# A Mamba-2 mixer with a LoRA mixture layer: all y and B of paired groups turned by VectorE, and its order beside GpSimd's splits rewritten

## The reference

```python
x = hidden; xn = layernorm(x)
proj = xn @ in_proj_w.T                    # gate 4096 | x 4096, B 1024, C 1024 | dt 64
xBC = silu(causal_conv4(hbc))              # 4 taps along time
dt_p = softplus(dt + dt_bias); dA = exp(dt_p * -exp(A_log))
state = state * dA + (dt_p * x) B^T        # per head (64 heads of 64, 8 groups, N = 128)
y = state C + x * D
yn = y * rsqrt(mean(y*y over the group's 512) + eps) * norm_weight * silu(gate)
out = x + yn @ out_proj_w.T + (xn @ W_base.T + b_base + top-2 LoRA mixture of 8 experts, rank 16)
```

## Time and profile before

| | |
|---|---|
| median of 3 runs | 3144.78 us (3144.62 to 3144.9) |
| profiled execution | 3145.09 us |
| its span, first to last instruction | 3143.4 us |
| granted TensorE clock | 1.0 over nearly the whole span |
| busy: PE, PEld, DVE, ACT, POOL | 99%, 82%, 81%, 54%, 27% |
| chain that ended last | PE 95%, DVE 2%, ACT 1%, DMA 1% |
| DMA | 672.63 MB, 214 GB/s |

### The profile page before, as it was taken

The page is one execution under the profiler, slowest core; times in us unless marked ns, Lnnn a source line. Parts: engine busy times, 40 slices in busy tenths (PEclk is TensorE's granted clock), DMA queues, the critical chain, the costliest instruction groups (busy, mean ns, idle before and its releaser), DMA issues.

```text
span 3143.4 us, 55218 instructions
## 1 busy us (share of the span) xinstructions
PE 3126.1 (99%) x17660; PEld 2573.4 (82%) x17660; DVE 2558.5 (81%) x4599; ACT 1704.5 (54%) x4467; POOL 835.5 (27%) x917
## 2 busy tenths in 40 slices
PE   8999999999999999999999999999999999999999
PEld 7788888887888888888788888888878888888887
DVE  7977777785589999999648999999954988989983
ACT  5766666664265555656226555556533655565551
POOL 4444434433022222222103222222210222222220
PEclk9999999999999999999999999999999999999999
DMA  8777777777665555555566555555546555555554
GB/s 290 274 265 272 264 276 266 261 256 263 232 216 194 189 201 187 189 194 201 173 225 205 191 191 191 201 184 190 209 166 236 196 195 187 195 194 201 186 189 161
DMA packets 185668, 672.63 MB, mean 214 GB/s; under 512 B 21056, under 2 KB 22208, under 8 KB 185408
## 3 DMA queue, kind: packets, MB, share of 16 engines
q1 hardware_dynamic: 161280, 584.91, 53.3%
q10 hardware_dynamic: 24128, 84.42, 7.6%
HBM read 532.41 MB, written 136.84 MB: 213 GB/s over the span
## 4 chain that ended last, share of the span: by engine, by line
PE 95%; DVE 2%; ACT 1%; DMA 1%; issue 0%; SPq 0%; POOL 0%; ACTq 0%; DVEq 0%; POOLq 0%
PE dense L1072 21%; PE dense L1074 21%; PE dense L1073 21%; PE pX L1072 7%; PE pX L1074 7%; PE pX L1073 6%; PE pY L1187 3%; PE pD L1217 1%; PE pD L1187 1%; DVE conv_us L1497 1%; PE pCB L1163 1%; PE pU L1072 1%; PE pS L1073 1%; PE pS L1072 1%; PE pS L1074 1%; PE pU L1074 1%
## 5 line engine op out<-in xcount | busy, mean ns | idle before, releaser
L1072 PE MATMUL dense<-xn_hi,w_hl 128*128 128x512 f32 (+2 forms) x2192 | 869.7, 397 | 0.8 <-POOL w_hl L444 0.5
L1074 PE MATMUL dense<-xn_hi,w_hl 128*128 128x512 f32 (+2 forms) x2192 | 853.7, 389 | 0.0
L1073 PE MATMUL dense<-xn_lo,w_hl 128*128 128x512 f32 (+2 forms) x2192 | 852.0, 389 | 0.0
L1497 DVE SCALAR_TENSOR_TENSOR conv_us<-conv_in,const_g,conv_us 128x512 f32<-128x512 f32 x576 | 480.3, 834 | 47.0 <-ACT conv_us L694 33.2
L1074 PEld LDWEIGHTS dense<-xn_hi,w_hl 128*128 128x128 f32 (+1 forms) x2192 | 409.5, 187 | 88.9
L1072 PEld LDWEIGHTS dense<-xn_hi,w_hl 128*128 128x128 f32 (+1 forms) x2192 | 409.9, 187 | 86.0 <-issue 2.2
L1073 PEld LDWEIGHTS dense<-xn_lo,w_hl 128*128 128x128 f32 (+1 forms) x2192 | 410.3, 187 | 83.5 <-issue 1.2
L1072 PE MATMUL dense<-z_hi,w_hl 128*128 128x512 f32 x820 | 324.4, 396 | 1.6 <-DVE acc L1680 1.1
L501 POOL TENSOR_TENSOR C_lo<-BC,C_hi 128x128 fp32r<-128x128 f32 x120 | 60.0, 500 | 983.5 <-ACT S_hi L736 982.9
L1074 PE MATMUL dense<-z_hi,w_hl 128*128 128x512 f32 x820 | 319.7, 390 | 0.0
L1073 PE MATMUL dense<-z_lo,w_hl 128*128 128x512 f32 x820 | 319.1, 389 | 0.0
(11 more groups left out here) (233 smaller groups left out, 5935.3 us busy)
## 6 DMA issues: line engine op xcount, KB each, us to landing
w_hl<-w_split SPq DMA_DIRECT2D x732, 512.0 KB, 3.5
w_split<-w_hl SPq DMA_DIRECT2D x244, 512.0 KB, 3.8
cum_b<-cum_scratch ACTq DMA_DIRECT2D x128, 512.0 KB, 4.9
w_raw<-w_slots_dram SPq DMA_DIRECT2D x122, 512.0 KB, 5.4
acc<-x_tr_dram ACTq DMA_DIRECT2D x16, 512.0 KB, 6.5
out_tr_dram<-acc ACTq DMA_DIRECT2D x16, 512.0 KB, 4.7
BC<-x_tok_dram SPq DMA_DIRECT2D x6, 512.0 KB, 5.3
conv_us<-x_tok_dram SPq DMA_DIRECT2D x6, 512.0 KB, 6.2
```

The lines of the kernel that those rows point to most:

```text
L1072: nc.tensor.matmul(out, lhs[0], rhs[0], start=start, stop=False)
L1073: nc.tensor.matmul(out, lhs[0], rhs[1], start=False, stop=False)
L1074: return nc.tensor.matmul(out, lhs[1], rhs[0], start=False, stop=stop)
L1497: nc.vector.scalar_tensor_tensor(out=conv_u[r], in0=conv_in[r][:, t:t + TB], scalar=const_g[p][:, 4 * j + t:4 * j + t + 1], in1=conv_u[r], ...
```

## The change

- x, B and C of a group lie in one tensor (`xBC`), and so do their token rows: `x_rows` turns x and B in one instruction, 320 elements wide, where `x_rows` had 256 and `B_rows` 128. `B_rows` is gone.
- y of chunks 2 and 3 of paired groups is turned by VectorE too, in its own group (`yn_rows(g, p, 2, ...)`), and gated and split as a pair. TensorE's `chunk_3` is left for block 0 and for group 0.
- `chunk_1_x` and `chunk_1_cb` of paired groups fall into `wx_product`, `dtx_product`, `b_low` and `cb_masked`, ScalarE's `chunk_1` into `b_high`, `cs_high`, `ramps` and `wx_high`, and the conv taps into single calls; the order on VectorE, ScalarE, GpSimd and TensorE is written anew around them.
- On GpSimd the inverse roots of a pair are one addition and one power on two columns (`inv_rms_pair`), and the decay of chunk 2 comes behind them.

The diff, cut to its core (what is the same call under another name is left out):

```diff
 w_hl = [sb(f"w_hl{i}", [128, 2, 2, 512], F32R) for i in range(2)]
-xT = [sb(f"xT{i}", [128, XT, TB]) for i in range(2)]
-BC = [sb(f"BC{i}", [128, 2, TB]) for i in range(2)]
+xBC = [sb(f"xBC{i}", [128, XT + 2, TB]) for i in range(2)]
+xT = [t[:, 0:XT, :] for t in xBC]
+BC = [t[:, XT:XT + 2, :] for t in xBC]
...
-    def chunk_pre(g, p, c):
+    def chunk_pre(g, p, c, low_only=False):
...
         ins.then_inc(cs_lo, 1)
+        if not low_only:
+            decay(g, c)
+
+    def decay(g, c):
         if not (last_block and c == NC - 1):
+            S_c = state_at(g, c)
             pool.wait_ge(cs_lo, carry_n(q, g, c, first_block))
             nc.gpsimd.tensor_tensor(S_cur[:].rearrange("n (h p) -> n h p", h=HPG),
...
-    def inv_rms(g, c, two=False):
-
-        r = half_of(two, c)
+    def inv_rms_pair(g, c):
+
+        n = chunk(q, g, c)
+        pool.wait_ge(sq_done, n + 2 + 1)
+        nc.gpsimd.tensor_tensor(rstd[:, :, 0], ssq[:], eps_t[:, 0:1].broadcast_to([128, 2]), ALU.add).then_inc(rstd_done, 2)
+        pool.wait_ge(rstd_done, n * 2 + 2)
+        nc.gpsimd.tensor_tensor(rstd[:, :, 1], rstd[:, :, 0], eps_t[:, 1:2].broadcast_to([128, 2]), ALU.pow).then_inc(rstd_done, 2)
+
...
         wx_low(g, 0)
         chunk_pre(g, p, 1)
         wx_low(g, 1)
-        inv_rms(g, 0, True)
-        inv_rms(g, 1, True)
-        chunk_pre(g, p, 2)
+        chunk_pre(g, p, 2, low_only=True)
+        inv_rms_pair(g, 0)
         wx_low(g, 2)
+        decay(g, 2)
         chunk_pre(g, p, 3)
         wx_low(g, 3)
         if last and not last_block:
             ln_inv(q + 1, 0)
             ln_inv(q + 1, 1)
-        inv_rms(g, 2, True)
-        inv_rms(g, 3, True)
...
+    def b_high(g, c, two=False):
+        n = chunk(q, g, c)
+        if two:
+            act.wait_ge(xt_done, xt_n(q, g, c))
+            act.wait_ge(st_done, upd_n(q, g, c, last_block) - 1)
+        else:
+            act.wait_ge(s1, n * 2 + 2)
+        nc.scalar.activation(B_hi[:], x_tm[:, c % 2, GC:GC + N] if two else pCB[:, 0:N], ACT.Copy).then_inc(ck_evac, 1)
+
+    def cs_high(g, p, c):
+        if first_block and c == 0:
+            return
+        if c == 0:
+            act.wait_ge(post, post_n(q, g, NSET - 1))
+        nc.scalar.activation(C_hi[:], CT[p][:, c * Q:(c + 1) * Q], ACT.Copy)
+        act.wait_ge(s_upd, grp(q, g) * S_STEPS + (c + 2 if c else 1))
+        nc.scalar.activation(S_hi[:], state_at(g, c), ACT.Copy).then_inc(cs_hi, 1)
+
...
+    def chunk_3(g, c, after_router=False):

         n = chunk(q, g, c)
         if after_router:
             pe.wait_ge(rt_dve, q * RT_DVE + 9)
         pe.wait_ge(z_done, n * 2 + (4 - 1))
-        if two:
-            pe.wait_ge(y_done, n - c % 2 + (2 + 1))
         pe.wait_ge(yn_done, n + 1 + 1)
         for j in range(XT):
             mm = nc.tensor.transpose(pD0[:, j * 128:(j + 1) * 128], yn[c % 2][:, j * 128:(j + 1) * 128], ident[:])
-        mm.then_inc(s3, 3 if two and c == 2 else 1)
+        mm.then_inc(s3, 1)


...
         j = 0
         gate_unit(g, False, 0, True)
-        if second:
-            chunk_3(g - 1, 2, two=True)
         gate_unit(g, False, 1, True)
+        gate_unit(g, False, 2, True)
+        if not second:
+            chunk_3(0, 3)
         chunk_1(g, 0, p, True, True)
-        gate_unit(g, False, 2, True)
-        chunk_3(g - 1, 3, two=second)
         gate_unit(g, False, 3, True)
+        out_units(g, 0, two=True)
         chunk_2s(g, 0)
         chunk_2b(g, 0)
-        out_units(g, 0, two=True)
+        out_units(g, 1, two=True)
         chunk_1(g, 1, p, True, True)
-        out_units(g, 1, two=True)
         if last:
...
+    def conv_tap(g, j, p, t):
+
+        r, n = j % 2, (post_n(q, g + 1, j) - 1) * 3
+        if t == 0:
+            if j == 0:
+                dve.wait_ge(consts_ready, q * PREPS + (1 if g is NO_GROUP else g + 2))
+            dve.wait_ge(evac_act, act_n(q, g, 4 + j))
+        else:
+            dve.wait_ge(taps, n + t)
+        nc.vector.scalar_tensor_tensor(out=conv_u[r], in0=conv_in[r][:, t:t + TB],
+                                       scalar=const_g[p][:, 4 * j + t:4 * j + t + 1], in1=conv_u[r],
+                                       op0=ALU.mult, op1=ALU.add).then_inc(taps, 1)
+
...
             for k in range(4):
-                src = xT[p][32 * f:32 * f + 32, :, :].rearrange("n j (c t) -> n j c t", c=NC)
-                dst = x_tm[32 * k:32 * k + 32, :, :].rearrange("p c (j i) -> p j c i", j=XT)
+                src = xBC[p][32 * f:32 * f + 32, 0:XT + 1, :].rearrange("n j (c t) -> n j c t", c=NC)
+                dst = x_tm[32 * k:32 * k + 32, :, :].rearrange("p c (j i) -> p j c i", j=XT + 1)
                 ins = nc.vector.transpose(dst[:, :, :, 32 * f:32 * f + 32], src[:, :, c:c + 2, 32 * k:32 * k + 32])
         if end == 4:
             ins.then_inc(xt_done, 1)
...
+    def wx_product(g, c):
+        if last_block and c == NC - 1:
+            return
+        if c == 0:
+            dve.wait_ge(prep_done, q * PREPS + g + 2)
+        dve.wait_ge(xt_done, xt_n(q, g, c))
+        nc.vector.tensor_tensor(heads(wx[:]), heads(x_tm[:, c % 2, 0:GC]), per_head(1, c), ALU.mult).then_inc(xw_done, 1)
+
+    def dtx_product(g, c):
+        dve.wait_ge(xt_done, xt_n(q, g, c))
+        nc.vector.tensor_tensor(heads(dtx_2[c % 2]), heads(x_tm[:, c % 2, 0:GC]), per_head(0, c), ALU.mult)\
+            .then_inc(xw_done, 2 if last_block and c == NC - 1 else 1)
+
+    def b_low(g, c):
+        dve.wait_ge(ck_evac, chunk(q, g, c) + 1)
+        nc.vector.tensor_tensor(B_lo[:], x_tm[:, c % 2, GC:GC + N], B_hi[:].bitcast(F32), ALU.subtract)\
+            .then_inc(bl_done, 1)
+
+    def cb_masked(g, c):
+        dve.wait_ge(s1, chunk(q, g, c) * 2 + 2)
+        nc.vector.tensor_tensor(CBm, pCB[:, N:N + Q], causal[:], ALU.mult).then_inc(cbm_done, 1)
+
...
+    def yn_rows(g, p, c, first, end):

         if first == 0:
-            dve.wait_ge(yn_done, chunk(q, g, 1) + 1 + 1)
+            dve.wait_ge(yn_done, chunk(q, g, c) + 2 + 1)
         for f in range(first, end):
             for k in range(4):
                 src = yn_2[32 * k:32 * k + 32, :, :].rearrange("t c (j i) -> t j c i", j=XT)
-                dst = xT[p][32 * f:32 * f + 32, :, 0:2 * Q].rearrange("n j (c t) -> n j c t", c=2)
+                dst = xT[p][32 * f:32 * f + 32, :, c * Q:(c + 2) * Q].rearrange("n j (c t) -> n j c t", c=2)
                 ins = nc.vector.transpose(dst[:, :, :, 32 * k:32 * k + 32], src[:, :, :, 32 * f:32 * f + 32])
         if end == 4:
             ins.then_inc(yt_done, 1)

-    def gated_pair(g, p):
+    def gated_pair(g, p, c):
+        cs = slice(c * Q, (c + 2) * Q)
         dve.wait_ge(gate_done, grp(q, g) * XT + XT)
-        dve.wait_ge(yt_done, (q - 1) * (G - 1) + g)
-        z = xT[p][:, :, 0:2 * Q]
-        nc.vector.tensor_tensor(z, z, gate[:, :, 0:2 * Q], ALU.mult).then_inc(z_done, 2)
-
-    def gated_lo_pair(g, p):
-        dve.wait_ge(zhi_done, chunk(q, g, 0) + 2)
-        nc.vector.tensor_tensor(z_lo[:, :, 0:2 * Q], xT[p][:, :, 0:2 * Q],
-                                z_hi[:, :, 0:2 * Q].bitcast(F32), ALU.subtract).then_inc(z_done, 2)
+        dve.wait_ge(yt_done, yt_n(q, g, c))
+        nc.vector.tensor_tensor(xT[p][:, :, cs], xT[p][:, :, cs], gate[:, :, cs], ALU.mult).then_inc(z_done, 3)
+
+    def gated_lo_pair(g, p, c):
+        cs = slice(c * Q, (c + 2) * Q)
+        dve.wait_ge(zhi_done, chunk(q, g, c) + 2)
+        nc.vector.tensor_tensor(z_lo[:, :, cs], xT[p][:, :, cs], z_hi[:, :, cs].bitcast(F32), ALU.subtract)\
+            .then_inc(z_done, 1)

...
+        x_rows(g, 0, p, 0, 1)
+        if second:
+            silu(g - 1, 5, p)
+            gated_lo_pair(g - 1, 1 - p, 2)
+            prep(g)
+            x_rows(g, 0, p, 1, 3)
+            gate_tile(g, 0, False)
+            gate_tile(g, 1, False)
+            x_rows(g, 0, p, 3, 4)
+            wx_product(g, 0)
+            b_low(g, 0)
+        else:
+            x_rows(g, 0, p, 1, 4)
+            wx_product(g, 0)
+            b_low(g, 0)
+            gated(0, 3)
+            gated_lo(0, 3)
+            gate_tile(g, 0, False)
+            gate_tile(g, 1, False)
+        dtx_product(g, 0)
+        gate_tile(g, 2, False)
+        cb_masked(g, 0)
         masked(g, 0, True)
-        gate_tile(g, 2, False)
+        gate_tile(g, 3, False)
+        dve.wait_ge(acc_loaded, (q + 1) * 64)
+        out_adds(g, 0, halves=(0,), two=True)
         if last:
             router_weights()
+        out_adds(g, 0, halves=(1,), two=True)
         y_state(g, 0, True)
+        state(g, 0)
+        wx_product(g, 1)
         y_skip(g, 0, True)
-        gate_tile(g, 3, False)
-        state(g, 0)
-        dve.wait_ge(acc_loaded, (q + 1) * 64)
-        chunk_1_x(g, 1, True)
-        out_adds(g, 0, halves=(0,), two=True)
+        b_low(g, 1)
+        dtx_product(g, 1)
+        out_adds(g, 1, halves=(0,), two=True)
         x_rows(g, 2, p, 0, 1)
-        out_adds(g, 0, halves=(1,), two=True)
-        x_rows(g, 2, p, 1, 2)
```

(48 more changed lines are left out.)

280 lines of the change are left out of this document (130 added, 150 removed).

## The result

The changed kernel takes 3174.78 us (median of four, 3173.83 to 3175.45), the kernel before beside it 3144.84: a ratio of 1.0093, with a 95% interval of 1.0076 to 1.0111. I had forecast 3131, with a range that ended at 3160. The profiled execution has a span of 3172.9 us and a time of 3174.59, where the kernel before had 3143.4 and 3145.09.

What follows compares the result with a forecast made beforehand. TensorE's matmul issue was taken as the bound in blocks 1 to 3: 19.3 us saved, 5.4 given back to stalls because VectorE's round is 88.2 against 87.2, so -13.9 from 3145.09 gives 3131; range 3125 to 3160.

Steps and rivals of the forecast that it cites:

- What leaves TensorE: 42 chunk_3 calls in blocks 1 to 3, 0.46 us each, saving 19.3 us; group 87.2, block 3 86.5.
- The turns: On VectorE per group: sixteen more of y +7.2, B's gone -5.0, x grown to 0.51 each +2.1.
- VectorE's own work, 81.9: VectorE's operations in one paired group, without any stretch from GpSimd: 85.9 less 4.0 us.
- New waits, 4.8: VectorE per group: 2.6 us for B_hi at b_low, 1.4 and 0.8 at the turns of y.
- Contention, "so I take half, 1.5": VectorE's stretch beside GpSimd per group: between 0 and 2.9 us, taken as 1.5.
- all three meetings of the walk: VectorE beside GpSimd: gate_tile(2) up to 1.2, sum with xD and dtx of chunk 3 up to 1.4, B_lo 0.3.
- my upper end: The most stretch foreseen for VectorE in a group, all meetings with GpSimd paid in full: 2.9 us.
- the forecast's own formula: Stall per block: VectorE's round over TensorE's pace, times some 5.5 rounds, less 3 us of slack.
- What being late costs: TensorE stalls after 3 us of lateness: 2.7 us in blocks 1 and 2 each, none in block 3; 5.4 given back.
- two rivals: VectorE as bound (3162, chance 0.27; block 3 stall 4 us); meetings only move (3148, chance 0.13; block 3 stall 2).
- The rival that VectorE becomes the bound: Stretch stays 4.0, VectorE's round is 90.7, 17 us slower: 3162; decided from a round of 89.5; chance 0.27.
- Today's waits fall away, since they end when TensorE or ScalarE come to them: VectorE's waits for the evacuation (1.6 us) and z_hi (1.3) were said not to come from its own chain.

Runs made afterwards that it cites:

- run 5: The changed kernel with B_lo of chunk 0 behind the masks and eight idle TensorE transposes per paired group: 3141.3 us, 0.9989 of the kernel before.
- run 3: The kernel before, with one instead of four TensorE transposes in each of the 42 chunk_3 calls of paired groups: 3141.3 us, ratio 0.9988.
- run 1: The changed kernel with VectorE's B_lo of chunk 0 behind the masks (groups 2 to 7, blocks 1 to 3): 3128.2 us, 0.9949 of the kernel before.
- run 6: The changed kernel with gate_tile(2) ahead of B_lo of chunk 0: 3150.1 us, 1.0017 of the kernel before.
- run 4: The changed kernel with ScalarE's B_hi and wx_hi of chunk 0 ahead of gate evacuation 3 (groups 2 to 7): 3161.0 us, ratio 1.0051.

## Why the prediction was wrong, by its own steps

- *What leaves TensorE*: right. 176 records of the turns are left; a round at full supply takes 87.12 (forecast 87.2), in block 3 86.4 (86.5); a call is worth 0.43 or 0.44 in runs 5 and 3, where 0.46 was read.
- *The turns*: right. The grown turn of x takes four in 2.06, 0.51 each; a turn of y 0.44.
- *VectorE's own work, 81.9*: 0.6 too low. The round of 90.03 less 5.3 of waits and 2.2 of stretch leaves 82.5.
- *New waits, 4.8*: 0.5 too low. B_lo waits 2.45 (forecast 2.6), the turns of y 1.49 and 1.35 (1.4 and 0.8). The chain from `gate_tile(0)` through ScalarE came out as it was walked.
- *Contention, "so I take half, 1.5"*: 0.7 too low, the largest of the three terms. The usual round has all three meetings of the walk: 0.32 at a B_lo, 0.84 at dtx of chunk 3, 1.06 at `gate_tile(2)`, 2.2 together. The third round of block 1 has 3.4, over my upper end, since the sum with xD and the product were both stretched there. Which way that place falls was luck. The gate tile's meeting had no luck in it: its two times both follow from the wait that I had worked out, 2.6, and so it deserved its full 1.2. A mean of possible meetings is not an estimate of one that the computed times make certain.
- The three together, 0.6 + 0.5 + 0.7, turn 88.2 into 90.0, and every term erred to the same side. This mis-sized round is the first step that failed. By the forecast's own formula the 0.7 alone would have made it some 3142, and the measured rounds, 90.0 and 88.4, some 3160 (estimates): 34 us given back against 19.3, the edge of the range.
- *What being late costs*: "late by some 3 us before TensorE stops" is the second step that failed, and it takes the time out of the range: 48 us were given back, not 34 (18.3, 17.1 and 13.0 in blocks 1 to 3, against run 1). I took VectorE to be at its sums of y when TensorE ends `chunk_2y`; it is 2.3 us behind there in normal running, and the margin at pU is 0.5. (No row shows the half a microsecond that the forecast took off for semaphores; in run 3 TensorE starts 0.11 behind the SiLU it waited for.) Nor is the number of rounds 5.5: five rounds of block 1 are over TensorE's pace. Against 87.1, and 87.6 for the last of them (run 1), they give back 16.3 us, 1.3 of it in the third, with its longer stretch, and the last stretch, in group 7, another 2.2. My formula with the right round, (90.03 - 87.12) x 5.5 - 3, would have given 13; six rounds, the 1.1 of the longer meeting and 0.5 of slack give 18.1. A stall also costs TensorE more than the list of waits shows: in the window 1239.26:1329.29 it waits 2.3 us and is also busy for 87.71, 0.6 more than in a round without a wait. In block 3 the round was 88.4, not the forecast 87.0, and "no stall" there was wrong too.
- *The sums*: 5.5 less 3 is 2.5, not 2.7, which moves the forecast by 0.4. The terms for block 3 in two rivals, 4 and 2 us, don't follow from the -1.2 of the main case. By it the rival with 90.7 has 89.5 in block 3 and (89.5 - 86.5) x 5.5 - 3 = 13.5 us of stall, and comes to some 3172. The measured round of block 3 is 1.6 below that of block 1.
- *The rival that VectorE becomes the bound* had the mechanism and the sign, with a chance of 0.27, and the round went past its point of decision, 89.5. It took the stretch of the kernel before, 4.0, where it was 2.2 with larger work and waits; and it had the same slack of 3 us, without which its 3162 would have been nearer to the result.
- *"Today's waits fall away, since they end when TensorE or ScalarE come to them"*: the waits for the evacuation and for z_hi are gone in the changed order. But run 3 speaks against it as a reading of the kernel before, where VectorE's chain was within some tenths of TensorE's pace with these waits in it.
- The Trainium skill's advice against this change ("VectorE: DVE Perf Modes", "Rules for kernel authors": a 128x128 transposition goes to TensorE where PSUM will do as its destination) is right for the order as changed and not for this kernel in general: with B_lo moved the kernel with these turns on VectorE is 0.5% faster than the kernel before, and 36 idle calls put back on TensorE cost it 13.1 us (run 5), for as long as VectorE's round stays under 87.1.

## What to carry to other kernels

When work moves from the engine that sets the time to the next busiest, write the next one's round as work plus waits for third engines plus meetings, and compare it with the first one's new pace: here 90.0 against 87.1, and a microsecond of any of the three kinds was worth 0.9 to 1.0 in the round. A wait in the middle of an in-order engine also shifts everything behind it, so look at what the shifted operations run into. The cure may be one line: put what needs a late input behind what doesn't, as far as it still comes ahead of the last of its consumer's inputs. Read the slack for that at the consumer, as the time between its last input and its start, and not from an engine's position elsewhere.

## What the runs showed of the hardware

- At the sum with xD of chunk 3 the meeting of VectorE with GpSimd is decided by hundredths of a microsecond and falls on one of two values, 0.84 or 1.98 us in all at the same place of the program (run 6), so rounds of one kernel differ by 1.1 to 1.2 us with the same instructions. GpSimd pays when it comes second: the decay 1.59 instead of 1.05.
- A stall of TensorE can be followed by a lower clock. In the changed kernel's third round it stops for 2.42 us ahead of 1184.15. By windows of 3 us (columns as above) the granted clock goes from 1.00 to 0.59, then 0.84, and back:

```profile
1181.00:1184.00 3.00, 0.74 (x26) 0.60 (x22) 3.00 (x6) 2.63 (x9) 0.00 (x0) 1.00 0.38 145
1184.00:1187.00 3.00, 2.85 (x35) 2.56 (x36) 2.93 (x6) 0.12 (x1) 0.00 (x0) 0.59 0.02 5
1187.00:1190.00 3.00, 3.00 (x12) 2.39 (x12) 2.90 (x6) 1.93 (x5) 0.00 (x0) 0.84 0.00 0
1190.00:1193.00 3.00, 3.00 (x15) 2.49 (x14) 2.93 (x6) 1.34 (x4) 1.30 (x2) 1.00 0.47 178
```

and the timeline has the matmuls of that stretch at the level of 1.2 GHz, 0.43 us from start to start, and then again at 0.23:

```profile
1186.35 0.63 PE L1125 MATMUL dense<-xn_lo,w_hl 128*128 128x512 f32 x1
1186.78 0.63 PE L1126 MATMUL dense<-xn_hi,w_hl 128*128 128x512 f32 x1
...
1188.03 0.39 PE L1126 MATMUL dense<-xn_hi,w_hl 128*128 128x512 f32 x1
1188.26 0.40 PE L1124 MATMUL dense<-xn_hi,w_hl 128*128 128x512 f32 x1
```

  Rounds with the same 2.3 us in two waits of 1.2 and 1.1 kept a clock of 1.00, and so did a round of run 4 with a single stall of 2.40 ahead of 1182.74. So the length of the stall alone doesn't decide it. No run was made for the clock alone, and what in a stall brings it down stays open here.
